# Other places for the late stages of the last bands, and VectorE takes band 2's second norm

## The reference

```python
x = layernorm(x + attention(x) @ out_w.T + out_b)          # 16 heads, softmax(q k / sqrt(8) - slope * distance) v
l1 = ln(x); qkv = l1 @ qkv_weight.T                         # block: 2 positions attend causally
h = x + softmax(scores) v @ proj_weight.T                   # "hidden after attention"
n = ln(h)                                                   # second norm; goes to router and experts
p = softmax(n @ router_weight); top 2; rank of each row within its expert, slot = expert * 640 + rank
moe = sum over the two experts of p * (gelu(n @ w1) @ w2)   # rows are scattered to xd, results to yt
out = layernorm(x + h + moe)
```

## Time and profile before

| | us |
|---|---|
| median of three runs (lowest, highest) | 625.75 (624.24, 625.88) |
| the profiled execution's own time | 627.75 |
| its span | 625.9 |
| busy: PE / DVE / ACT / POOL | 528.1 / 404.5 / 346.1 / 220.3 |
| unit loop from 433 to 465.2: PE, DVE, ACT, POOL busy | 26.26, 17.87, 21.68, 12.21 of 32.20 |
| TAIL, 465.2 to 512.9 | 12.16, 23.41, 8.39, 21.54 of 47.70 |

### The profile page before, as it was taken

The page is one execution under the profiler, slowest core; times in us unless marked ns, Lnnn a source line. Parts: engine busy times, 40 slices in busy tenths (PEclk is TensorE's granted clock), DMA queues, the critical chain, the costliest instruction groups (busy, mean ns, idle before and its releaser), DMA issues.

```text
span 625.9 us, 11852 instructions
## 1 busy us (share of the span) xinstructions
PE 528.1 (84%) x4498; PEld 297.8 (48%) x4498; DVE 404.5 (65%) x698; ACT 346.1 (55%) x679; POOL 220.3 (35%) x406
## 2 busy tenths in 40 slices
PE   6579999999999999989999999999872309999910
PEld 4224444444444555444455555655542207888710
DVE  3587786878888686998857789867537422222217
ACT  4237675767677776766866766776841112332404
POOL 5635554111325143025505003620254520545540
PEclk9698999999999999999999999999985557999975
DMA  7632352222322222212123321110000011442124
GB/s 156 157 94 76 76 140 79 83 82 88 111 82 80 96 82 89 90 57 62 56 68 93 91 75 32 40 41 3 19 9 22 28 53 33 139 127 84 57 79 135
DMA packets 49192, 47.90 MB, mean 77 GB/s; under 512 B 13251, under 2 KB 38709, under 8 KB 49136
## 3 DMA queue, kind: packets, MB, share of 16 engines
q1 hardware_dynamic: 40800, 31.93, 18.7%
q0 software_dynamic: 5488, 12.73, 6.8%
q10 hardware_dynamic: 2848, 2.49, 1.2%
HBM read 31.67 MB, written 16.06 MB: 76 GB/s over the span
## 4 chain that ended last, share of the span: by engine, by line
PE 68%; DVE 14%; DMA 7%; issue 4%; ACT 3%; POOL 2%; ACTq 1%; SPq 0%; POOLq 0%; DVEq 0%
PE ps L894 32%; PE ps L941 16%; DVE row_max L1346 6%; PE ps L1089 5%; PE ps L1077 5%; PE ps L896 4%; DMA max_dram<-max_turned 1%; PE ps L967 1%; ACT probs L1194 1%; DMA k_stacks<-k_dram 1%; DVE heads L1399 1%; POOL xd L781 1%; DVE x_tok L1553 1%; POOL yt L817 1%; PE ps L1066 1%
## 5 line engine op out<-in xcount | busy, mean ns | idle before, releaser
L1346 DVE TENSOR_REDUCE row_max<-ps 128x1 f32<-128x1024 f32 x256 | 296.9, 1211 | 89.7 <-PE ps L894 46.3
L1194 ACT ACTIVATE probs<-ps 128x512 f32<-128x512 f32 x512 | 268.8, 608 | 87.6 <-PE ps L896 47.2
L894 PE MATMUL ps<-k_stacks,q_stacks 96*128 96x512 bf16 x448 | 145.8, 391 | 13.7 <-DMA k_stacks<-k_late 5.3
L894 PE MATMUL ps<-q_stacks,k_stacks 99*128 99x512 bf16 (+1 forms) x512 | 142.4, 357 | 0.0
L941 PE MATMUL ps<-probs,v_unit 128*32 128x256 f32 x2048 | 124.7, 384 | 0.0
L896 PE MATMUL ps<-distance,slope_eye 128*128 128x128 bf16 x512 | 111.6, 223 | 0.0
L941 PEld LDWEIGHTS ps<-probs,v_unit 128*32 128x32 f32 x2048 | 60.1, 110 | 51.8 <-issue 10.2
L894 PEld LDWEIGHTS ps<-k_stacks,q_stacks 96*128 96x128 bf16 x448 | 39.5, 100 | 84.1 <-DVE row_max L1346 29.0
L894 PEld LDWEIGHTS ps<-q_stacks,k_stacks 99*128 99x128 bf16 x512 | 49.2, 99 | 39.6 <-ACT probs L1194 10.5
L896 PEld LDWEIGHTS ps<-distance,slope_eye 128*128 128x128 bf16 x512 | 50.9, 99 | 25.9 <-issue 2.4
L817 POOL DMA_INDIRECT yt<-prod_mix,y_to x40 | 38.9, 972 | 54.1 <-DVE prod_mix L1522 42.2
(11 more groups left out here) (195 smaller groups left out, 450.1 us busy)
## 6 DMA issues: line engine op xcount, KB each, us to landing
k_stacks<-k_dram SPq DMA_DIRECT2D x46, 144.0 KB
q_stacks<-q_dram SPq DMA_DIRECT2D x46, 72.0 KB
w<-in_w SPq DMA_DIRECT2D x12, 256.0 KB
xd<-blank POOLq DMA_DIRECT2D x8, 325.0 KB, 2.7
probs<-xd SPq DMA_DIRECT2D x8, 325.0 KB
k_stacks<-in_c_alibi_k SPq DMA_DIRECT2D x24, 96.0 KB
out_dram<-out_t SPq DMA_DIRECT2D x16, 128.0 KB
yt<-zeros POOLq DMA_DIRECT2D x4, 512.0 KB, 3.0
```

The costliest lines, as they stand in the source:

```text
L894: mm = pe.matmul(out, lhs, rhs, start=True, stop=at is None)
L1194: act.activation(probs[:, k % KEPT, HALF * e:HALF * (e + 1)], ps[:, ring_of(n), :], ACT.Exp).then_inc(ring_read, 1)
L1346: dve.tensor_reduce(row_max[:, m % 2, i:i + 1], max_pair(k).rearrange("p a n -> p (a n)"), AX.X, ALU.max).then_inc(mx_used, 1)
```

## The change

Four parts. The table gives bands 2 and 3 other places in halves 60 to 63; two stages, LOGITS 2 and ATT_T 3, stand in the middle of the last `values` group; TAIL has another order; and HID2 and X2 of band 2 go from GpSimd to VectorE. HID of bands 3 and 4 gets one more wait (that GpSimd has finished with the hidden rows of the band before the last), HID2 on VectorE waits for `x1_ready`, and the two norms get separate `stats` buffers. No instruction is added; the kernel's arithmetic is the same.

In halves, the moves are: EXP2 2 from 60.5 to 60.25, X2 2 from 62.25 to 62.5, HID2 2 from 62.25 to 62, T2 2 from TAIL to 63.5; PROJECT 3 from 60 to 60.5, HID 3, STATS0 3 and ROOT0 3 from 60 to 60.75, L1 3 from 61.5 to 62, T1 3 from 61.75 to 62.75, QKV_MM 3 from 62 to 63, SCORE 3 from 62 to 63.25, EXP2 3 from 62.5 to 63.5, MIX 3 from 62.5 to 63.75, ATT_T 3 from 63.25 to behind half 63, PROJECT2 3 from 63.75 to TAIL.

```diff
-     SCORE: 11.5, EXP2: 12.5, MIX: 12.5, ATT_T: 13.5, PROJECT2: 14, HID2: 14.25, STATS2: 14.25, ROOT2: 14.25, X2: 14.25},
+     SCORE: 11.5, EXP2: 12.25, MIX: 12.5, ATT_T: 13.5, PROJECT2: 14, HID2: 14, STATS2: 14.25, ROOT2: 14.25, X2: 14.5,
+     T2: 15.5},
...
+TAIL_FIRST = ((LOGITS, 2), (ATT_T, 3))
...
-                if stage == HID2 and c < SMALL:
+                if stage == HID2 and c < PER_S:
...
-                    if c < SMALL:
+                    if c < PER_S:
                         pool.wait_ge(rstd_ready[2], c + 1)
...
-                        for stage, c in hooks(half, (3,)):
+                        for stage, c in (hooks(half, (3,)) if half < HALVES else TAIL_FIRST):
                             late(stage, c)
...
-            for stage, c in TAIL:
+            for stage, c in TAIL[len(TAIL_FIRST):]:
                 late(stage, c)
...
                     dve.wait_ge(b_added, 1)
+                    dve.wait_ge(base_ready, c - 1)
...
-                if stage == HID2 and c >= SMALL:
+                if stage == HID2 and c >= PER_S:
                     dve.wait_ge(ring_read, LATE_PLACE[PROJECT2, c] + 1)
+                    dve.wait_ge(x1_ready, c + 1)
...
-                if stage == X2 and c >= SMALL:
+                if stage == X2 and c >= PER_S:
```

More of the change, by code:

```diff
@@ L91 @@
     {RECIP_A: 3, RECIP_B: 4, TURN: 5, PROJECT: 6, HID: 6, STATS0: 6, ROOT0: 7, X1: 7, L1: 9, T1: 10, QKV_MM: 11,
-     SCORE: 11.5, EXP2: 12.5, MIX: 12.5, ATT_T: 13.5, PROJECT2: 14, HID2: 14.25, STATS2: 14.25, ROOT2: 14.25, X2: 14.25},
-    {RECIP_A: 3, TURN: 3, PROJECT: 4, HID: 4, STATS0: 4, ROOT0: 4, X1: 5.25, L1: 5.5, T1: 5.75, QKV_MM: 6, SCORE: 6,
-     EXP2: 6.5, MIX: 6.5, ATT_T: 7.25, PROJECT2: 7.75},
-)
[L98 to L104, removed]
+     SCORE: 11.5, EXP2: 12.25, MIX: 12.5, ATT_T: 13.5, PROJECT2: 14, HID2: 14, STATS2: 14.25, ROOT2: 14.25, X2: 14.5,
+     T2: 15.5},
+    {RECIP_A: 3, TURN: 3, PROJECT: 4.5, HID: 4.75, STATS0: 4.75, ROOT0: 4.75, X1: 5.25, L1: 6, T1: 6.75, QKV_MM: 7,
+     SCORE: 7.25, EXP2: 7.5, MIX: 7.75},
+)
+TAIL_FIRST = ((LOGITS, 2), (ATT_T, 3))
+TAIL = TAIL_FIRST + ((LESS_MAX, 2), (EXP_LOGITS, 2), (PROJECT2, 3), (ROUTE_A, 2), (HID2, 3), (STATS2, 3), (ROOT2, 3),
+                     (ROUTE_B, 2), (X2, 3), (RANK, 2), (T2, 3), (RECIP_A, 4), (TURN, 4), (SLOT, 2), (PROJECT, 4),
+                     (LOGITS, 3), (HID, 4), (STATS0, 4), (ROOT0, 4), (LESS_MAX, 3), (EXP_LOGITS, 3), (X1, 4),
+                     (SCATTER0, 2), (SCATTER1, 2), (ROUTE_A, 3), (L1, 4), (T1, 4), (QKV_MM, 4), (ROUTE_B, 3),
+                     (SCATTER2, 2), (SCORE, 4), (RANK, 3), (SCATTER3, 2), (EXP2, 4), (MIX, 4), (ATT_T, 4), (PROJECT2, 4),
+                     (SLOT, 3), (HID2, 4), (STATS2, 4), (SCATTER0, 3), (ROOT2, 4), (X2, 4), (T2, 4), (SCATTER1, 3),
+                     (LOGITS, 4), (LESS_MAX, 4), (EXP_LOGITS, 4), (ROUTE_A, 4), (ROUTE_B, 4), (RANK, 4), (SLOT, 4),
+                     (SCATTER0, 4), (SCATTER1, 4))
 def units_of(c):
@@ L258, in body @@
         row_of = [sb(f"row_of{k}", [P, NT, XW]) for k in range(TOP)]
-        stats = sb("stats", [P, TC, 6])
+        stats = sb("stats", [P, 2, TC, 6])
         mv = [sb(f"mv{i}", [P, NT, 2]) for i in range(3)]
@@ L1365, in norm_stats @@
                 for j in range(width(c)):
-                    last = dve.bn_stats(stats[:, j, :], src[:, j, :])
+                    last = dve.bn_stats(stats[:, i, j, :], src[:, j, :])
                 done(last)
                 for j, a in enumerate(tiles(c)):
-                    last = dve.bn_aggr(mv[i][:, a, :], stats[:, j, :])
+                    last = dve.bn_aggr(mv[i][:, a, :], stats[:, i, j, :])
                 last.then_inc(var_ready[i], 1)
```

## The result

| | before | after |
|---|---|---|
| median of 20 runs each (lowest, highest), us | 625.82 (624.08, 629.11) | 621.37 (619.44, 626.01) |
| ratio, 95% interval | | 0.9926 [0.9907, 0.9945] |
| profiled execution: own time / span | 627.75 / 625.9 | 624.08 / 622.3 |

The account below looks back on a forecast made before the run. TensorE and ScalarE are nearly full until 465.2 us; then TAIL's chain of short engine-to-engine steps sets the end. Terms -0.3 - 2.1 + 1.75 - 1.4 = -2.1 us take 625.75 to 623.6 us, range 622.3 to 626.2.

Parts of the forecast that it names:

- Term 1: Last attention values: by ScalarE's new chain they end at 464.8 rather than 465.13 us, 0.3 us earlier.
- lower bound of -0.6: End of the values: what 18 handoffs could win if ScalarE's rows overlap by 0.05 to 0.1 us at each change.
- Term 2: Values to LESS_MAX 2: LOGITS 2 is done inside the values, only keep_out and a copy follow; 2.1 us earlier.
- Term 3: VectorE from LESS_MAX 2 to RECIP_A 4: 6.59 us of work instead of 4.84, so 1.75 us later.
- wait for the heads: Before RECIP_A 4: the heads' load lands near 470.5 us, stays hidden, and would hold a gain above 2.2 us.
- Term 4: GpSimd in TAIL: ROOT0 4 follows STATS0 4 by 0.1 us instead of 1.50, without two scatters ahead; 1.4 us earlier.
- the cover of 0.5 us on GpSimd: GpSimd's wait for SLOT 3 before band 3's scatters: 3.0 - 2.5 = 0.5 us left after the later scatters, enough.
- The effect that I weighed by the rule: ROOT0 4's two roots beside VectorE work, contending for SBUF: 2 x 0.16 = 0.3 us back, left out of the sum.
- Rival 1: Clock falls at the last values, behind ATT_T 3's gap: 0.9 us more, gain 1.2, time 624.5 us; chance 0.15.
- rival 2: The clock fall at 458 us is absent from the timed runs: gain only 0.4, time 625.3 us; chance 0.17.
- Rival 3: GpSimd's scatter queue holds up ROOT2 4 and takes the 1.4 us back: time 625.0 us; chance 0.05.
- rival 4: Slower: the loop's end becomes a single-file chain with clock falls, values 4.0 us late, time 627.9 us; chance 0.08.

Follow-up runs that it names:

- the pair of LOGITS kernels: T2 2 and LOGITS 2 moved into unit 31 and the last values in before alone: -0.2 us; put back behind the values in after: -2.3 us, both against before.
- ROOT0 4 first: Before with ROOT0 4 and X1 4 put ahead of SCATTER0 2 in TAIL: -1.2 us (-2.6, +0.2) against before.

## Why the prediction was wrong, point by point

| term | predicted | measured |
|---|---|---|
| 1. end of the values | -0.3 | -1.40 |
| 2. values to LESS_MAX 2 | -2.1 | -2.20 |
| 3. LESS_MAX 2 to RECIP_A 4 | +1.75 | +1.30 |
| RECIP_A 4 to STATS0 4 ends | 0 | +0.06 |
| 4. STATS0 4 to ROOT0 4 | -1.4 | -1.42 |
| ROOT0 4 to the last scatter | 0 | -0.05 |
| sum | -2.1 | -3.71 |

The mechanism was right at each of the three points, and so was the sign; the size was not. Of the 2.5 us by which the forecast fell short, 1.6 are in terms 1 and 3, and 0.9 are not found at a place. With the 1.6 the forecast would have been 622.0, still above the 621.37 measured.

**Term 1 failed.** The step that failed is the sum of row durations along ScalarE's chain: it gave 0.3 for the end of the values, which came 1.4 earlier. From EXP2 2 at 441.57 to the end of ATT_T 2's copy at 448.77 went 7.20 us, where I had added up 7.69; on to EXP2 3 13.02, where I had 13.49; from there to the end of the values 4.09 against 4.01, handoffs apart; and the 0.24 for six handoffs was in the measured stretches already. Together 1.1, over 18 durations. All waits stood where I had put them: 1.01, 1.10 and 1.32 us on TensorE before PROJECT2 2, QKV_MM 3 and ATT_T 3 (forecast: about 1.3 each), 1.86 before EXP2 2 (forecast: 2). Nor was a part of the clock left out: the sum runs along the new chain, in which the granted clock is 1.00 up to the end of the values. The lower bound of -0.6 had the right sign and half the size: I allowed 0.05 to 0.1 for the overlap of two rows, and the rows after show 0.14 (0.39 to 0.25), 0.19 (0.86 to 0.67) and 0.21 (4.03 to 3.82) at one change of row. The starts would have told: in before's own eight exponentials of 4.03 begin at 437.28 and the next row at 441.11, 3.83 later, 0.48 for each and not 0.504.

**Term 2 held** as a sum (0.56 behind the values), but its worth hangs on the rest: the pair of LOGITS kernels shows 1.6 net in the new order and, by the estimate above, 0.3 in the old.

**Term 3** was 0.45 too large, for more than half of it by the same error on VectorE: LESS_MAX 2 0.70 (0.75), ROUTE_A 2 2.01 (2.20), HID2 3 with STATS2 3 1.14 (1.25), ROUTE_B 2 1.77 (1.79), X2 3 0.52 (0.60). In the 2.20 one product of 32 columns took 0.40 us, which takes 0.19 elsewhere; that 0.2 was chance. The rest are ends taken where starts count. No wait for the heads came, as forecast.

**Term 4 held**, shown from both sides, and the cover of 0.5 us on GpSimd held with it: the scatters of band 3 begin 0.86 us behind SLOT 3, as in before, and ROOT0 4 to the last scatter is the same to 0.05. The effect that I weighed by the rule (the Trainium skill, GPSIMD Engine Reference, section Specifications) and sized at 0.3 did not come: ROOT0 4's two roots took 0.72 and 0.71 us, as the 0.71 of the earlier trace rows. But I had their neighbours wrong. LESS_MAX 3 was over at 478.05, before the first root began at 478.22, and X1 4 began behind the first and ended ahead of the second; only ROUTE_A 3's short products of 0.2 us ran beside the second. Where the change did move such a root is ROOT0 3 (its second root, L729 of before): beside MIX 2's products of two inputs it took 0.87 us in all six executions of kernels built on before, and 0.71 with VectorE idle in all eight of kernels built on after, which agrees with the rule. It wins no time: L1 3, which needs it, begins 1.3 us or more behind it in both.

**The rivals.** Rival 1 didn't come: both matmul groups of the last values ran at full clock (16 took 1.07 us, as in before), and the clock fell only behind them. Against rival 2 stands that the fall at +24 was there in all three executions with before's loop unchanged (before twice, ROOT0 4 first), and a gain far above its 0.4; and such a fall, which I had priced at 1.7, cost 1.2 in the two executions where it can be priced. Rival 3 and rival 4 didn't come.

**What stays open.** The 3.7 us at the last scatter lie inside the interval of the time (3.4 to 5.8), but in 10 of the 12 comparisons the measured gain is larger than the one at the last scatter, by 0.75 on the mean. One profiled execution per kernel shows that the stretches ahead of +0 and behind the last scatter vary by several us, and can't show whether their mean differs. Over all fourteen profiled executions the stretch from the last scatter to the end has a median of 111.5 us in the six of kernels built on before and 111.2 in the eight of kernels built on after, so at most 0.3 seems to lie there. I could not place the rest. Nor is it shown what the new places of PROJECT 3, L1 3, T1 3 and QKV_MM 3 are worth by themselves, since no kernel moves them alone; the 1.13 us that TensorE waited for PROJECT 3 are gone with them.

## What to carry to other kernels

Along a chain on one engine, add up start to start, from rows of the same shape that stand in a row, never durations: over 18 rows the difference was 1.1 us, half of the forecast. Count every place from a mark just ahead of the change, and two executions of one kernel whose spans differ by 5.6 us agree to 0.1. And weigh an edit only in the order in which it will stand: the same move of LOGITS 2 was worth some 0.3 or 1.6 us, the same move of a norm cost 3.7 us or nothing, by whether something else waited there.

## What the runs showed of the hardware

Of TensorE's idle times in halves 60 to 63 and the last values: at 2.55 or 2.56 us in four executions and at 5.91 in one, the granted clock fell to 0.50 each time; at 1.99 to 2.00 us it fell in two executions and stayed at 1.00 in four; at 2.10 us it stayed once, and at 1.01 to 1.52 us always. So the same idle time in the same order is sometimes followed by a fall and sometimes not, and such a fall (about 3.4 us at half clock) cost 1.2 us in both executions where it could be priced. Before with ATT_T 3 late, behind its 1.99 us:

```profile
441.80:442.30 0.50, 0.50 (x4) 0.38 (x4) 0.42 (x2) 0.50 (x2) 0.00 (x0) 1.00 0.04 10
442.40:442.90 0.50, 0.50 (x9) 0.27 (x12) 0.00 (x0) 0.50 (x2) 0.00 (x0) 0.50 0.00 0
```

The 2.10 us, of after with LOGITS 2 behind the values:

```profile
466.29 0.44 PE L982 MATMUL ps<-ident,l 128*128 128x128 f32 x2 [2.10 <-DVE l L1444]
466.65 1.07 PE L943 MATMUL ps<-probs,v_unit 128*32 128x256 f32 x16
```

The value matmuls behind it take 1.07 us for 16, as at full clock.
